# Twelve slots instead of eight for gathered rows in a four-layer graph network

## The reference

```python
h = relu(layernorm(x)); x = x + L0(h)   # Z = h @ W;  relu(segment_sum(Z[src] * weight, dst))
h = relu(layernorm(x)); x = x + L1(h)   # Z = h @ W.T + b, normed by degrees; relu(segment_sum(.., dst))
h = relu(layernorm(x)); x = x + L2(h)   # a = h + segment_sum(h[src], dst); relu(a @ W1 + b1) @ W2 + b2
h = relu(layernorm(x)); x = x + L3(h)   # 8 heads: Wx = h @ Ws + Wb; softmax over each dst's edges; sum alpha * Wx[src]
```

## Time and profile before

| | us |
|---|---|
| median of 3 runs (lowest, highest) | 3579.93 (3575.55, 3582.34) |
| the profiled execution | 3570.49 |
| its span, first to last instruction | 3569.2 |
| pass 0 (window 188 to 842) | 654 |
| pass 1 (870 to 1503) | 633 |
| pass 2 (1518 to 2163) | 645 |
| pass 3 (2920 to 3562) | 642 |
| mean granted clock of TensorE | 0.838 |

### The profile page before, as it was taken

How to read it: one execution, slowest core, us unless ns; L and a number is a source line. 1 busy time by engine, 2 the same in 40 slices (tenths; PEclk the granted TensorE clock), 3 DMA queues, 4 the chain that set the end, 5 groups by cost and what they waited for, 6 DMA issues and landing times.

```text
span 3569.2 us, 32096 instructions
## 1 busy us (share of the span) xinstructions
PE 2501.9 (70%) x8214; PEld 1315.9 (37%) x8214; DVE 1648.3 (46%) x3871; ACT 225.0 (6%) x418; POOL 1945.6 (55%) x2038
## 2 busy tenths in 40 slices
PE   2878888886777777678787786111267757888887
PEld 1634444332222222234444444101245534444444
DVE  3565565542344333323433433000157776666665
ACT  1400000000000000000000000000000010000000
POOL 0066666664666666566666663777300026666665
PEclk9989999998888999869988897555655569999999
DMA  2276666665666666566666662000032126666665
GB/s 100 82 235 192 177 181 177 208 214 153 192 187 204 194 204 195 158 186 178 182 179 179 180 182 56 12 9 12 23 109 97 37 64 187 193 187 192 188 193 166
DMA packets 200815, 539.21 MB, mean 151 GB/s; under 512 B 52446, under 2 KB 53735, under 8 KB 200660
## 3 DMA queue, kind: packets, MB, share of 16 engines
q0 software_dynamic: 149568, 463.26, 44.5%
q1 hardware_dynamic: 49934, 71.57, 6.0%
q10 hardware_dynamic: 1158, 2.33, 0.2%
HBM read 504.13 MB, written 32.90 MB: 150 GB/s over the span
## 4 chain that ended last, share of the span: by engine, by line
PE 47%; issue 13%; DMA 12%; DVE 11%; another core or an unknown queue 9%; POOL 6%; SPq 2%; ACT 0%; DVEq 0%; POOLq 0%; ACTq 0%
PE tiles L1267 28%; DMA ring<-table,src_t 9%; POOL ring L1530 6%; PE upper L1230 4%; PE tiles L1264 3%; PE tiles L1265 2%; PE last_bank L1230 2%; PE last_bank L1411 2%; DMA acc<-dst_places 2%; PE upper L1269 1%; PE upper L1219 1%; SPq L1594 1%; DVE ring L1063 1%; DVE big L955 1%
## 5 line engine op out<-in xcount | busy, mean ns | idle before, releaser
L1530 POOL DMA_INDIRECT ring<-table,src_t x1760 | 1681.2, 955 | 1352.7 <-issue 405.2
L1267 PE MATMUL tiles<-ring,sel 128*125 128x512 f32 x2640 | 1440.8, 663 | 317.3 <-issue 168.1
L1267 PEld LDWEIGHTS tiles<-ring,sel 128*125 128x125 f32 x2640 | 460.6, 201 | 817.6 <-issue 808.4
L418 DVE TENSOR_TENSOR sel<-iota_bank,dl_t 128x500 f32<-128x500 f32 (+1 forms) x330 | 222.8, 676 | 749.2 <-PE tiles L1267 243.4
L1063 DVE TENSOR_TENSOR ring<-ring,last_bank 128x512 f32<-128x512 f32 x440 | 293.3, 684 | 201.9 <-DMA ring<-table,src_t 165.5
L1561 POOL DMA_INDIRECT big<-score_table,src_t x264 | 259.0, 981 | 129.1 <-issue 83.7
L1264 PE MATMUL tiles<-ring,sel 128*125 128x512 f16 x440 | 198.0, 450 | 108.5 <-DMA ring<-table,src_t 63.1
L1269 PEld LDWEIGHTS upper<-big,sel 128*125 128x125 f32 x880 | 172.5, 196 | 227.4 <-issue 227.3
L660 DVE TENSOR_SCALAR sel<-node_iota,dl_t,w_t 128x125 f32<-128x125 f32 x440 | 145.4, 354 | 235.2 <-PE tiles L1267 165.9
L1230 PE MATMUL upper<-wh,hTh 128*125 128x512 f32 x252 | 127.8, 507 | 169.5 <-DVE hTl L899 119.9
L1230 PE MATMUL last_bank<-wh,hTh 128*125 128x512 f32 x148 | 71.3, 482 | 181.6 <-DVE hTl L899 94.3
(11 more groups left out here) (289 smaller groups left out, 2374.1 us busy)
## 6 DMA issues: line engine op xcount, KB each, us to landing
ring<-table,src_t POOLq DMA_INDIRECT x1760
table<-stage SPq DMA_DIRECT2D x75, 250.0 KB
acc<-dst_places SPq DMA_DIRECT2D x55, 250.0 KB
x<-in_x SPq DMA_DIRECT2D x25, 250.0 KB
table<-acc SPq DMA_DIRECT2D x25, 250.0 KB
out<-x SPq DMA_DIRECT2D x25, 250.0 KB
acc<-src_places SPq DMA_DIRECT2D x22, 250.0 KB
x<-in_x SPq DMA_DIRECT2D x4, 1250.0 KB
```

Of the source, the lines that this page charges most:

```text
L418: V.tensor_tensor(to, iota_p[:, None, :].to_broadcast([CE, SB, TN]), dl_t[:, i:i + SB, None].to_broadcast([CE, SB, TN]), ALU.is_equal).the ...
L1267: last = P.matmul(to, sel[:, i % SELS, :], ring[:, r, :], start=False, stop=True, skip_group_check=True)
L1530: G.indirect_dma_start(out=(ring16 if layer == 2 else ring)[:, n % RING, :], out_offset=None, in_=table[layer][:, :], in_offset=bass.Indir ...
```

## The change

`RING` becomes 12 and all twelve slots take gathered rows. `STAGED` is gone. `SELS` stays 8. Since 440 is no multiple of 12, the slot of a step is now counted through all layers. The raw weights `raw_w` and `raw_wh` move to `big`, 4*FW to 8*FW; `row8` moves from 6*FW to 4*FW and `aw_bc` from 4*FW to 8*FW. `row8` and `raw_w` now share a place, so SyncE loads `G1_in` no longer ahead of pass 1 but inside it, ahead of the seventh float16 row store (`G1_AT`), once the flags are done. `WEIGHTS_AT` becomes 150, `WS_AT` 9 and `G2_AT` 15.

```diff
-    RING = 8
-    STAGED = 12
+    RING = 12
...
-    WEIGHTS_AT = 136
-    WS_AT, G2_AT = 8, 14
+    WEIGHTS_AT = 150
+    G1_AT, WS_AT, G2_AT = 6, 9, 15
...
-    assert RING == SELS == LOADED and DEG_END + 3 * TILES < STEPS
-    assert STAGED >= RING + KB
+    assert SELS == LOADED and DEG_END + 3 * TILES < STEPS
+    assert RING >= 7 + KB
...
-        ring = sb("ring", [CE, STAGED, D])
+        ring = sb("ring", [CE, RING, D])
...
-        raw_w = flat_ring[:, RING * D:(RING + KB) * D].rearrange("p (k d) -> p k d", k=KB)
+        raw_w = big[:, 4 * FW:4 * FW + KB * D].rearrange("p (k d) -> p k d", k=KB)
...
-        row8 = big[0:H, 6 * FW:6 * FW + 4 * (STEPS + 2)].rearrange("p (a i) -> p a i", a=4)
+        row8 = big[0:H, 4 * FW:4 * FW + 4 * (STEPS + 2)].rearrange("p (a i) -> p a i", a=4)
...
-        raw_wh = flat_ring[:, RING * D:(RING + KB) * D].rearrange("p (k h j) -> p k h j", k=KB, h=H)
-        aw_bc = big[:, 4 * FW:4 * FW + 2 * D].rearrange("p (s h j) -> p s h j", s=2, h=H)
+        raw_wh = big[:, 4 * FW:4 * FW + KB * D].rearrange("p (k h j) -> p k h j", k=KB, h=H)
+        aw_bc = big[:, 8 * FW:8 * FW + 2 * D].rearrange("p (s h j) -> p s h j", s=2, h=H)
...
-                r = i % RING
+                r = n % RING
...
             S.wait_ge(w_turned, KB)
-            S.dma_start(raw_w, G1_in.rearrange("(k p) d -> p k d", p=128)).then_inc(w_in_sb, 16)
             S.wait_ge(pj_out, 2 * TILES)
...
             for k in range(TILES):
+                if k == G1_AT:
+                    S.wait_ge(flags, 1)
+                    S.dma_start(raw_w, G1_in.rearrange("(k p) d -> p k d", p=128)).then_inc(w_in_sb, 16)
                 if k == WS_AT:
```

## The result

The changed kernel took **3588.4 us** (median of 20 runs, 3576.9 to 3601.2) beside 3581.4 us for the kernel before (20 runs): ratio 1.0027 [1.0015, 1.0039], about 10 us slower by the ratio and 7 us between the medians. The forecast was 3543 us (37 us faster), between 3470 and 3615: the range held the time, the sign was wrong. The profiled execution took 3586.4 us.

The account below looks back on a forecast made before the run. No engine was busy throughout; the four gather passes, 72% of the span, lost 349 us to GpSimd's pauses for free slots. Terms -35 - 2.2 + 0.5 gave -37 us, so 3543 us, range 3470 to 3615.

Parts of the forecast that it names:

- The reading of the kernel before: Four gather passes: gathers 1.25 us apart, then pauses of some 2 us awaiting late step messages, 349 us together.
- part (1): Gather passes: a ring of 12 lengthens runs of gathers between pauses, -35 us, bounded by nothing and all 349.
- the 10 of the forecast: Gather passes: runs grow from 9 to about 10 gathers between pauses, cutting 349 us to 314.
- a lag that follows the ring: Gather passes: if messages wait for GpSimd's pause, run length and lag are one thing; would break the forecast most, unpriced.
- bound of 131 us: Gather passes: TensorE's waits for rows, 131.3 us without two first gathers, all that earlier rows could return directly.
- The matrices cut in earlier: Gather passes: eight selection-matrix slots limit runs to about 10 gathers, not 11.4; so 35 us less, not 73.
- Part (2): Boundary of passes 0 and 1: moving the 1024 KB load G1 away saves 2.2 us, between 0 and 4.5.
- The +0.5 us for the load inside pass 1: Pass 1: G1's 1024 KB now load beside the gathers, costing 0.5 us, between 0 and 3.5.
- Part (3): Big buffer: second product's raw weights, aw and flag rows change place with the same instructions and no new wait; nothing.
- Nothing returns: Rival, chance 0.22: in the gather passes matrix slots replace the ring's limit, or pauses await no slots; 3578 us.
- the pauses are no wait for slots: Gather passes: second cause offered for no gain, GpSimd's pauses not being waits for free ring slots; shares chance 0.22.
- Slower: Rival, chance 0.18: in the gather passes longer runs delay messages, TensorE stands and falls to 1.2 GHz; 3622 us.

Follow-up runs that it names:

- r8: Changed kernel with only eight of its twelve slots used by the gathers, weights at their new places: 3584.9 us, ratio 1.0004.
- s12r11: Changed kernel with eleven slots for gathered rows and twelve for selection matrices instead of eight: 3586.5 us, ratio 1.0005.
- ring12_b: The changed kernel itself, timed again beside the kernel before in another session: 3598.3 us, ratio 1.0039.
- ring12_score1: Changed kernel with one tiny GpSimd memset and a wait after each score gather between third and fourth pass: 3514.0 us, ratio 0.9792.
- s12r8: Changed kernel with eight slots for gathered rows and twelve for selection matrices: 3585.7 us, ratio 0.9996.
- tell4: Changed kernel with TensorE counting up its step semaphore by four at every fourth step, a quarter of the messages: 3646.1 us, ratio 1.0180.
- apart_b: Changed kernel with gathers waiting only for their own landings in four slots, steps on fixed zero slots: 4953.8 us; the same file as apart, 2983.7 us.

## Why the prediction was wrong

**The reading of the kernel before** held: 1.25 us from gather to gather, pauses of some 2 us at the end of runs, late messages that arrive together, and 349 us of pauses; also, in part, that "messages come through when GpSimd pauses", which stood only in a rival.

**The step that failed is part (1), "the loss per gather is the pause over the run"**, with a pause of fixed size after a run that grows with the ring. Measured from the traces, pauses over 1 us and the sum of all pauses (beyond 0.305 us a gather): before 194 and 350 us, changed kernel 187 and 349, r8 196 and 358, s12r11 202 and 366. Runs went from 9.1 to 9.4 gathers, toward the 10 of the forecast, and each pause grew with them, so that the loss stayed 0.2 us a gather. For the sum of pauses is nearly an identity, a pass's time less 440 x 1.25 us, and no cause: whatever sets the pass sets the pauses. Four more slots let GpSimd get four steps further ahead once in a pass, 4 x 1.45 = 5.8 us, and the pass then goes on at the old pace. Of this, 1.2 to 2.1 us went into the lag, from a step's end to the gather that it frees (medians of the gathers that waited: 3.7, 5.4, 5.9 and 5.2 us before, 5.1, 7.0, 7.1 and 7.3 now), and the rest into rows that lie in the ring longer. The prediction named as what would break it most "a lag that follows the ring" and gave it no price. Its bound of 131 us, TensorE's waits for rows, was no bound of a gain either: 56 us of them went away, and the time stayed.

**"The matrices cut in earlier"** was the reason for taking 10 and not 11.4. It is not so either: with twelve matrices the passes keep their time. VectorE's 243 us for steps were, like its 165.5 us for landings, waits that can be moved or kept without a gain.

**Part (2)**, G1 moved: from the last step of pass 0 to the first of pass 1 it took 29.15 us and takes 27.6 (forecast -2.2, measured -1.6, on one trace each). The chain's pieces there in the changed kernel:

```profile
865.66 5.72 DMA table<-acc
872.26 4.85 DMA ring<-table,src_t
```

The first gather lands 1.5 us sooner than the earlier trace rows have it, the store not at all. The +0.5 us for the load inside pass 1 was too small to be seen. **Part (3)**, nothing: right by r8.

**The rivals.** "Nothing returns" is nearest in size (3578). Of its two causes the matrices are refuted; the other, that "the pauses are no wait for slots", comes near: they are waits for slots, but from eight slots up their sum does not follow the number (350, 366 and 349 us with 8, 11 and 12; six slots have 398). "Slower" had the sign, and its premise (messages come when GpSimd pauses) is shown in part: they come faster then, and not only then; its price, TensorE running out at the lower clock, is not.

**Why it is 10 us slower stays open.** Twelve slots were slower in both sessions in which they were timed against eight (1.0027 and 1.0039), and r8 was not (1.0004). The three profiled kernels with twelve slots (changed, ring12_b, ring12_score1) have 665.0, 635.4, 646.0 and 642.4 us as means of the passes, before and r8 656.8, 633.0, 644.4 and 641.8. That is +8.2 in pass 0 and +4.6 in the others, less 1.6 at the boundary: 11 us. But this rests on one trace of each kernel, and single traces spread as widely: pass 0 took 652.5 us before and 661.0 in r8 and s12r8, all with eight slots, and 659.9 in the changed kernel. Pass 0, with a matrix a step, is the one that suffered from coarser messages in tell4 too. That a longer lag costs there is a guess, and eleven slots with twelve matrices cost nothing (s12r11), which fits it but does not prove it. What sets 1.45 us a gather in the passes, where messages and gathers must share, also stays open.

## What to carry to other kernels

Before a pause is priced, ask whether it is a cause or what is left over when a fixed issue time is taken from a pace set elsewhere; a deeper buffer gave nothing here, where the pace was set outside it. One run in which the steps and the gathers do not wait for each other (apart_b) tells the two apart. When one wait disappears from the list and another of the same length appears in the same pass, nothing was gained. Long legs of equal length in the chain that end in "another core or an unknown queue" (here eight of 32.6 to 32.9 us in a row, two more of 27 and 31) deserve the first look: the 190 us of that stretch are some twenty times what the change moved.

## What the runs showed of the hardware

- In apart_b TensorE's messages reached VectorE one per 11.2 us, and up to 81 us after their step, while indirect gathers were issued every 1.34 us; a step took 1.13 us when none were. The message from VectorE to TensorE arrived within 1.6 us beside the same gathers. Three memsets of 0.12 us after each gather, with a wait for each, removed the hold in the stretch between passes.
- Chip 11 ran the kernel before in 2939.6 us in one session and 3586.3 in another. In the quick sessions the hold was absent (apart 2983.7, apart_b 4953.8). What differs was not found. One mark: the quick traces hold every record of the step semaphore (440 a pass), the slow ones 318 to 379 a pass in the kernel before.
- An indirect gather of 128 rows took GpSimd some 0.945 us (0.94 to 0.98 as means of a pass) and 0.305 us to the next, whether it fetched 64, 256 or 512 columns of a row.
- The port of VectorE and GpSimd that the Trainium skill names (page "SBUF — State Buffer", section "SBUF: two separate sides") and by which VectorE can lock GpSimd out does not explain the held messages: in apart_b VectorE stood idle for 39.73 us in one piece while they were held.
